# Written out instead of looped: heads 1 to 14 of the attention stage of a transformer block, on all five engines

## What is computed

```python
q = (x @ Wq).reshape(B, T, H, dh).transpose(0, 2, 1, 3)
k = (x @ Wk).reshape(B, T, H, dh).transpose(0, 2, 1, 3)
v = (x @ Wv).reshape(B, T, H, dh).transpose(0, 2, 1, 3)
logits = jnp.einsum('bhqd,bhkd->bhqk', q, k)
logits = (logits + causal[None, None] + _pos_bias(rel_pos_bias, T)[None]) / dh
probs = jax.nn.softmax(logits, axis=-1)
out = jnp.einsum('bhqk,bhkd->bhqd', probs, v)
out = out.transpose(0, 2, 1, 3).reshape(B, T, H * dh)
return out @ Wo + bo
```

## Time and profile before

| | |
|---|---|
| median of 3 runs | 845.35 us (843.19 to 845.69) |
| the profiled execution | 844.46 us |
| its span from first to last instruction | 842.7 us |
| granted TensorE clock, mean | 0.975 of full |
| PE busy | 771.5 us (92%) |
| DVE busy | 707.7 us (84%) |
| ACT busy | 612.8 us (73%) |
| POOL busy | 298.9 us (35%) |
| head 0's first scores | at 52.13 us |
| the loop over heads 1 to 14 | 86.08 to 541.21 us |

### The profile page before, as it was taken

One profiled execution on the slowest core, in us unless ns is written; L12 is line 12 of the kernel. 1 busy time (PEld: TensorE's weight loads), 2 busy tenths in 40 slices (PEclk: granted clock), 3 DMA queues, 4 the chain that ended last, 5 costly groups with the idle time before them and its releaser, 6 DMA issues.

```text
span 842.7 us, 17198 instructions
## 1 busy us (share of the span) xinstructions
PE 771.5 (92%) x4436; PEld 657.1 (78%) x4436; DVE 707.7 (84%) x1596; ACT 612.8 (73%) x1340; POOL 298.9 (35%) x323
## 2 busy tenths in 40 slices
PE   3877999999999999999999999996489999999992
PEld 2656988888888888888889888885377777777771
DVE  5557888988888888888888888888778888898976
ACT  2356888887888888888788888873577767667672
POOL 2318823333332332333233233223503354445423
PEclk9899999999999999999999999999679999999997
DMA  7684334424423432442443343230003211122101
GB/s 279 219 280 89 75 66 97 88 62 87 100 62 76 95 77 62 93 94 62 87 95 67 70 97 82 62 75 26 25 1 129 76 60 43 46 75 75 51 1 50
DMA packets 56025, 70.72 MB, mean 84 GB/s; under 512 B 36032, under 2 KB 45120, under 8 KB 52544
## 3 DMA queue, kind: packets, MB, share of 16 engines
q1 hardware_dynamic: 55712, 69.83, 32.9%
q10 hardware_dynamic: 288, 0.59, 0.3%
HBM read 27.36 MB, written 9.50 MB: 44 GB/s over the span
## 4 chain that ended last, share of the span: by engine, by line
PE 75%; DVE 8%; issue 6%; POOL 4%; ACT 3%; DMA 3%; POOLq 0%; DVEq 0%; ACTq 0%; SPq 0%
PE out_ps L1191 16%; PE score_ps L1158 16%; PE trans_ps L1173 15%; PE shared_ps L1205 6%; PE trans_ps L1074 3%; PE score_ps L1074 3%; PE score_ps L1076 2%; PE score_ps L1075 2%; PE trans_ps L1075 2%; PE trans_ps L1076 2%; DVE pT_lo L961 2%; PE shared_ps L1074 2%; PE shared_ps L1076 2%; PE shared_ps L1075 2%; POOL rstd L421 1%
## 5 line engine op out<-in xcount | busy, mean ns | idle before, releaser
L649 ACT ACTIVATE probs<-score_ps,row_min 128x128 f32<-128x128 f32 (+7 forms) x256 | 189.9, 742 | 53.5 <-DVE row_min L848 53.4
L861 DVE TENSOR_TENSOR pT_lo<-trans_ps,pT_hi 128x512 fp32r<-128x512 f32 (+3 forms) x384 | 201.6, 552 | 16.7 <-ACT pT_hi L670 16.6
L670 ACT ACTIVATE pT_hi<-trans_ps 128x512 fp32r<-128x512 f32 (+3 forms) x384 | 185.1, 491 | 40.4 <-PE trans_ps L1173 28.8
L848 DVE CUSTOM_DVE_ANT_0 score_ps<-score_ps,bias 128x128 f32<-128x128 f32 (+7 forms) x256 | 194.6, 760 | 22.8 <-PE score_ps L1158 19.4
L1173 PE MATMUL trans_ps<-ident,probs 128*128 128x128 f32 x1152 | 190.0, 274 | 3.2 <-DVE pT_lo L861 1.8
L1158 PE MATMUL score_ps<-k_hl,q_hl 128*128 128x512 f32 (+2 forms) x768 | 182.5, 351 | 3.1 <-DMA k_hl<-k_hl 1.6
L470 POOL TENSOR_TENSOR acc<-acc,head_out 128x512 f32<-128x512 f32 x64 | 83.0, 1297 | 245.5 <-DVE head_out L879 245.3
L1173 PEld LDWEIGHTS trans_ps<-ident,probs 128*128 128x128 f32 x1152 | 136.8, 140 | 27.3 <-DVE pT_lo L861 11.9
L1191 PE MATMUL out_ps<-pT_hi,v_hl 128*128 128x512 f32 (+2 forms) x384 | 156.5, 409 | 1.1 <-DVE pT_lo L861 1.1
L961 DVE TENSOR_TENSOR pT_lo<-probs,pT_hi 128x512 fp32r<-128x512 f32 x144 | 133.2, 952 | 25.0 <-ACT pT_hi L728 15.1
L1158 PEld LDWEIGHTS score_ps<-k_hl,q_hl 128*128 128x128 f32 x768 | 134.4, 189 | 23.7 <-DMA k_hl<-k_hl 1.8
(11 more groups left out here) (122 smaller groups left out, 1163.3 us busy)
## 6 DMA issues: line engine op xcount, KB each, us to landing
q_hl<-k_hl SPq DMA_DIRECT2D x64, 256.0 KB, 3.6
k_hl<-k_hl SPq DMA_DIRECT2D x32, 512.0 KB, 4.2
v_scratch<-probs SPq DMA_DIRECT2D x16, 512.0 KB, 4.0
v_raw<-v_scratch SPq DMA_DIRECT2D x32, 256.0 KB, 4.6
bias_all<-gate_scratch SPq DMA_DIRECT2D x8, 1024.0 KB, 4.8
v_raw<-in_Wfc SPq DMA_DIRECT2D x8, 256.0 KB, 4.9
bias<-in_Wproj SPq DMA_DIRECT2D x8, 256.0 KB, 5.3
bias_all<-in_rel_steps SPq DMA_DIRECT2D x1, 1920.0 KB, 12.7
```

The source lines that it names most:

```text
L649: act.activation(probs[s % 4][:, 0:n], scores_of(s % QB)[:, 0:n], ACT.Exp, bias=row_min[:, s:s + 1], scale=-1.0, accum_out=row_sum[:, s:s ...
L670: act.activation(pT_hi[c][:, CH * g:CH * g + m, q * P:(q + 1) * P], trans_ps[k % 2][:, 0:m * P].rearrange("p (m q) -> p m q", q=P), ACT.Co ...
L848: dve.tensor_tensor_reduce(out=ps, in0=ps, in1=bias_b[b][:, T - n:T], scale=1.0, scalar=3e38, op0=ALU.add, op1=ALU.min, accum_out=row_min[ ...
L861: dve.tensor_tensor(pT_lo[c][dst], trans_ps[k % 2][:, 0:m * P].rearrange("p (m q) -> p m q", q=P), pT_hi[c][dst], ALU.subtract).then_inc(p ...
```

## The change

On each engine `with engine.Fori(1, H - 1) as h:` becomes a Python loop `for h in range(1, H - 1):`, so that the body stands 14 times in the program, with constants where registers were. No instruction that computes is added, removed or moved, nor any DMA.

```diff
@@ sync
-            with sp.Fori(1, H - 1) as h:
+            for h in range(1, H - 1):
                 head(h)
@@ gpsimd
-            with pool.Fori(1, H - 1) as h:
+            for h in range(1, H - 1):
                 for s in range(S):
                     slot(h, s, True, False)
@@ scalar
-            with act.Fori(1, H - 1) as h:
+            for h in range(1, H - 1):
                 for s in range(S):
                     slot(h, s, True, False)
@@ vector
-            with dve.Fori(1, H - 1) as h:
+            for h in range(1, H - 1):
                 for s in range(S):
                     slot(h, s, True, False)
@@ tensor
-            with pe.Fori(1, H - 1) as h:
+            for h in range(1, H - 1):
                 for s in range(S):
                     slot(h, s, True, False)
```

## The result

| | before | after |
|---|---|---|
| median, 20 runs each | 844.46 us (842.92 to 845.70) | 847.73 us (845.02 to 850.68) |
| ratio of the two | | 1.0036, 95% interval 1.0027 to 1.0044 |
| the profiled execution | 844.46 us | 846.44 us |
| its span | 842.7 us | 844.4 us |
| granted TensorE clock, mean | 0.975 | 0.977 |

The changed kernel is slower by 3.3 us in the medians. 847.73 stands beside the predicted 848.2; that forecast was built on a median before of 845.35 us from three runs, which came out at 844.46 over 20. In the two profiled executions the heads that were a loop took 3.50 us more; head 0 began 1.08 us earlier, took 0.04 more (34.00 against 33.96), and what follows head 15's start took 0.7 us less.

The account below looks back on a forecast made before the run. PE bounds the kernel (busy 389.97 of 390.04 us over heads 2 to 13). Waits add 0.23 us per head, times 14 = 3.2 us, other terms 0: 847.7 from the profiled execution, 848.5 from the median, forecast 848.2, range 844.8 to 851.0.

Parts of the forecast that it names:

- Part 1: Branch once per head and engine, 215 ns on PE: hidden by PE's queue, 0 gained, 3.0 us at the far end.
- Part 2: Register instructions at L1170 on PE (294) and L860 on DVE (308): they cost PE nothing, 0 gained.
- Part 3: Late waits moved ahead of their instructions: about 0.06 us each, 0.11 + 0.07 + 0.05 = 0.23 us more per head.
- for slot 9 ... I take slot 1's 0.05: Slot 9 of each head, without an undisturbed row: 0.05 us lost as in slot 1, bounded by 0 and 0.06.
- All heads alike: Sign in the profile after: slot 0 to slot 0 about 32.7 us instead of 32.50, the same in every head.
- Part 4: Fetching the written-out heads' code: 0 to 0.06 us per head, 0 to 0.8 us in 13 more heads, taken as 0.
- Nothing moves: Rival: the 0.11 us is head 15's alone or given back; 845.4 or 844.5 us; chance 0.26, including under 2 us.
- the loop's end costs: Rival: PE's branch at the body's end delays slot 0 by up to 0.215 us per head; 842.3 us; chance 0.07.
- Fetches are felt: Rival: 0.06 us per head, 849.3 us; 853 if delayed copies of k cost 5 half heads 1 us each; chance 0.12.

## Why the prediction was right, and where it was off

The direction, the place and the mechanism of the loss in each head were right. That the total came so close, 848.2 against 847.73, is partly luck: two wrong terms of 0.7 us each had opposite signs (parts 3 and 4).

**Part 1, the branch: right.** With all but PE written out, PE keeps its loop and the heads take 32.47 us, as with PE written out as well. No gap of PE was to be given back.

**Part 2, the register instructions: right.** The loop with all its waits in the good order takes 32.42 to 32.49 us per head, the written-out kernel with both swaps 32.47.

**Part 3, the waits that change places: the mechanism right, one term wrong.** The wait orders swapped back in the written-out kernel took the loss away, slot by slot. Predicted 0.11 in the first half, 0.07 in slot 15, 0.05 in slot 9, 0.23 us per head. Measured 0.06 in slot 1, 0.06 in slot 7, 0.06 in slot 15, nothing in slot 9, with the small rest 32.70 - 32.50 = 0.20 us, and 14 x 0.20 = 2.8. The step that failed is "for slot 9 ... I take slot 1's 0.05". The loss is there, but the loop had one of 0.06 us in the same slot already, at a pair of waits in the copy of k and q that stood the wrong way round in the loop and the right way round in constants. Since I had looked only for waits that the change makes worse, not for one that it mends, I missed it. "All heads alike" was wrong as well, by the next part.

**Part 4, the fetches: taken 0, measured 0.7 us.** Heads 1, 3, 7 and 11 are longer by 0.08, 0.24, 0.15 and 0.39 us than 32.70, and 458.63 - 14 x 32.70 = 0.8 us in all; the loop had 455.13 - 14 x 32.50 = 0.1. The 0.7 us between lie inside the bounds of 0 to 0.8, at the far end. ACT's two stalls are 2 x 0.23 of it, DVE's 0.17, the copies of k in head 11 and head 1 0.18 and 0.08. That the delays at the copies come from fetching PE's code is shown by their going together, and by moving that code; that ACT and DVE stall for their code is read from the places, every 128 instructions, and from the loops having none. They come not in equal parts per head, as the earlier trace rows had let me reckon, but in a few single stalls. The wrong zero of this part and the wrong 0.05 of slot 9 (0.7 us over 14 heads) made up for each other: predicted 3.2, measured 3.5 in the heads and 3.3 in the medians. The Trainium skill (Runtime: NRT & Kernel Launch, section Instruction fetch mechanics) names the stall only for a branch to code outside the window, and from it draws a preference for writing loops out. Here the loop's 14 branches bring no fetch, so the stall was not there to be saved, and reading the section as one fetch for each branch went too far. The written-out code is what has to be fetched.

**The rivals.** *Nothing moves* and *the loop's end costs* are out, by the 32.70 us and by the kernel with PE alone in a loop. *Fetches are felt* is true beside the forecast: two copies of k, with 1.4 us to spare, were delayed by 1.1 and 1.2 us. One of them, issued 0.24 us later in its head than the other, cost 0.18, and a third, issued 1.3 us late, cost 0.08, where the rival had put 1 us on five half heads. It was right to name the copy. In the changed kernel the delays were no longer than the time to spare, so that hardly anything of them reached PE. The same had happened in the kernel before: its copy issued at 112.97 (packet 1.22 us behind) took 5.5 us, landed at 118.5, and the next head began at 118.64; slot 15 of head 1 was 0.05 us too long, and that is most of the 32.56 of the earlier trace rows for which I had blamed fetching in general or the branch.

**Open.** Of the 2.3 us by which the written-out kernel with both swaps beats the one before in the medians (1.6 by the ratio), its profile shows 0.2 in the heads 1 to 14 (454.94 against 455.13) and 0.9 in the span. The rest isn't explained. The four kernels with ACT, DVE, POOL and SP written out and the good order of waits are at 0.9977 to 0.9986, the three that loop these engines and leave `split_hi` and `transpose_probs` their good order at 0.9995 to 1.0005. Yet the loop with `split_qk_hi` swapped as well takes 454.37 us for heads 1 to 14, and the four take 454.41 to 455.41. Whether writing out these engines gives something outside the heads is not shown either way.

## What to carry to other kernels

Where an instruction has two waits, one is taken ahead of it, and when that was the one that ended last, it cost about 0.06 us each time in this kernel, where PE's path was full. Turning a register loop into constants or back can reverse which one it is: read it from the built program, for waits made worse and waits mended alike, and set the order by the form. Writing the loop out gave nothing in the heads by itself. With the order set right the written-out kernel came to 0.9981 (0.9973 to 0.9990), and 0.9977 (0.9966 to 0.9987) with PE's code moved, of the kernel before, while the loop with its order set right is at 0.9995 (0.9984 to 1.0005); that difference is the open point above.

## What the runs showed of the hardware that I had not expected

- A 16 KB packet of code that starts 0.96 to 1.92 us behind a 512 KB copy's issue goes with a copy that lands after 4.9 to 6.1 us instead of 4.2 (24 of 24). A packet in the 0.6 us ahead of the issue does not, and with an 8 KB one 0.6 to 1.0 us behind it the copy takes 4.2 to 4.5. All of this is for the copies within the heads.
- ACT and DVE start an instruction some 0.3 us late at places that lie a multiple of 128 instructions apart (17 of 17, in nine kernels), with nothing in the profile that it could wait for; eight more instructions ahead move the place. PE then loses 0.17 to 0.23 us in most of them.
- The mean TensorE clock of the two profiles is 0.975 and 0.977, and 1.00 in the heads of both: PE was busy throughout, and neither loss shows in it.
